# Cross-attention of a two-layer decoder: score rounds of the filling in neighbouring pairs, and the last eleven shifted rounds in turn on two pairs of PSUM banks

## The reference

```
Q = (layernorm(x) @ Wq).heads   K = (ctx @ Wk).heads   V = (ctx @ Wv).heads
scores = einsum('bhqd,bhkd->bhqk', Q, K) * 0.25
attn = softmax(scores, axis=-1)
x = x + einsum('bhqk,bhkd->bqhd', attn, V).reshape(B, T, 256) @ Wo
```

## Time and profile before

| | |
|---|---|
| median of 3 runs | 1474.68 us (1469.47 to 1475.07) |
| profiled execution | span 1473.2 us from its first to its last instruction; a time of its own around the span is not given |
| cross-attention of layer 0 | 153.1 to 491.9 us |
| its first score round, first shifted round, last values | 163.5, 197.2, 479.4 us |
| cross-attention of layer 1 | from 942.0 us on |
| its first score round, first shifted round, last values | 952.2, 972.1, 1264.7 us |
| mean granted clock of PE | 0.911 |

### The profile page before, as it was taken

How to read it: one execution, slowest core, us unless ns; L and a number is a source line. 1 busy time by engine, 2 the same in 40 slices (tenths; PEclk the granted TensorE clock), 3 DMA queues, 4 the chain that set the end, 5 groups by cost and what they waited for, 6 DMA issues and landing times. The chain is left out here.

```text
span 1473.2 us, 34595 instructions
## 1 busy us (share of the span) xinstructions
PE 1305.0 (89%) x13568; PEld 1036.2 (70%) x13568; DVE 701.9 (48%) x1744; ACT 558.2 (38%) x1246; POOL 444.8 (30%) x654
## 2 busy tenths in 40 slices
PE   5998899999998389999994999799999998559996
PEld 2665457777776279999993777557777776459996
DVE  4885345555552612222222999545565552323322
ACT  2776035555554012222221555135555553112221
POOL 5994300000000155556552221200000000135662
PEclk8999579999998589999997999799999997569999
DMA  7000111111110369999984000011111110279994
GB/s 241 2 2 2 23 26 36 36 36 37 36 36 17 128 225 340 346 347 337 329 320 107 1 1 1 15 29 42 44 44 43 42 43 25 80 192 347 356 368 147
DMA packets 61355, 177.89 MB, mean 121 GB/s; under 512 B 20608, under 2 KB 41953, under 8 KB 46756
## 3 DMA queue, kind: packets, MB, share of 16 engines
q0 software_dynamic: 22176, 141.55, 27.0%
q1 hardware_dynamic: 39044, 34.46, 9.2%
HBM read 147.62 MB, written 12.85 MB: 109 GB/s over the span
## 5 line engine op out<-in xcount | busy, mean ns | idle before, releaser
L975 DVE TENSOR_REDUCE xa_mx<-xa_ps_s 112x2 f32<-112x750 f32 x246 | 231.5, 941 | 219.4 <-PE xa_ps_s L704 215.9
L892 ACT ACTIVATE xa_p<-xa_ps_p 125x672 f32<-125x672 f32 x256 | 187.2, 731 | 236.2 <-PE xa_ps_p L710 236.2
L710 PEld LDWEIGHTS xa_ps_p<-xa_qT,xa_kT 32*125 32x125 f32 x3072 | 199.4, 191 | 95.3 <-ACT xa_p L892 66.8
L710 PE MATMUL xa_ps_p<-xa_qT,xa_kT 32*125 32x112 f32 x3072 | 243.4, 291 | 24.4 <-DVE xa_mx L975 10.4
L704 PE MATMUL xa_ps_s<-xa_kT,xa_qT 32*112 32x375 f32 x984 | 224.8, 534 | 1.0 <-DMA xa_qT<-xa_qU 1.0
L1803 PEld LDWEIGHTS ex_ps_h<-ex_xT,ew_w 128*128 128x128 f32 x1792 | 213.7, 196 | 4.8 <-issue 2.0
L1803 PE MATMUL ex_ps_h<-ex_xT,ew_w 128*128 128x128 f32 x1792 | 214.3, 279 | 1.3 <-ACT ex_xT L1833 1.3
L1814 PE MATMUL ex_ps_y<-ew_w,ex_hT 128*128 128x256 f32 x896 | 202.7, 379 | 0.0
L1814 PEld LDWEIGHTS ex_ps_y<-ew_w,ex_hT 128*128 128x128 f32 x896 | 165.9, 190 | 20.2
L1837 ACT ACTIVATE ex_hT<-ex_ps_h,ew_w 128x128 f32<-128x128 f32 x224 | 70.1, 364 | 282.5 <-PE ex_ps_h L1803 282.5
L1849 DVE TENSOR_SCALAR ex_hT<-ex_ps_h,ew_w 128x128 f32<-128x128 f32 x224 | 68.2, 346 | 163.7 <-PE ex_ps_h L1803 163.7
(11 more groups left out here) (304 smaller groups left out, 2000.0 us busy)
## 6 DMA issues: line engine op xcount, KB each, us to landing
xa_kT<-xa_kU SPq DMA_DIRECT2D x128, 93.8 KB, 2.2
xa_qT<-xa_qU SPq DMA_DIRECT2D x64, 56.0 KB
xn<-xa_x SPq DMA_DIRECT2D x32, 112.0 KB, 2.2
lin_yg<-ys SPq DMA_DIRECT2D x16, 224.0 KB, 5.2
cT<-in_ctxT SPq DMA_DIRECT2D x4, 750.0 KB, 8.3
xa_qT<-xa_nmT SPq DMA_DIRECT2D x128, 1.8 KB
x<-in_x SPq DMA_DIRECT2D x4, 448.0 KB, 6.2
xn<-x SPq DMA_DIRECT2D x16, 112.0 KB, 2.1
```

Of the source, the lines that this page charges most:

```text
L710: return pe.matmul(bp[0:CT, i, c * S:(c + 1) * S], kT[r:r + 32, b % RB, n, c * CT:(c + 1) * CT], qT[r:r + 32, b % RB, n, :], start=True, s ...
L892: act.activation(p[slot % 4][:, :, :], bp[0:CT, :, 0:NC3 * S], ACT.Exp).then_inc(exped, 1)
L975: dve.tensor_reduce(mx[:, b % 2, j:j + 2, n], score_banks(b, pair)[0:S, :, 0:CL], AX, ALU.max).then_inc(maxed, 1)
```

## The change

Three edits and what they need:

1. **Filling.** `round_of` loses its branch without shifted rounds. The loop over t starts at 0, and the filling is written out ahead of it: `fill_round` in pairs 0 and 1, 2 and 3, and so on, with the other products between the pairs, and no identity product behind a round. `keys(0, 1)` stands ahead of the first round and of the five or nine identity products, which stay. On DVE `normed_row(1)` comes before the first maximum and `q_copy(1)` before the maximum of pair 4.
2. **Drain.** From round DRAIN = 117 on, the shifted rounds take `bsc` and `bp` in turn (`shifted_banks`) and wait for the exponential of two rounds before. Round 117 also waits for all 128 maxima.
3. **Zeros.** `spread_q` waits for `q_copied` behind its DMA of zeros instead of ahead of it.

```diff
+    DRAIN = PAIRS * NB - FILL
...
+    def shifted_banks(t, slot):
+
+        r = PAIRS * t + slot
+        return bsc if r >= DRAIN and (r - DRAIN) % 2 == 0 else bp
...
             def spread_q(b):
-                sp.wait_ge(q_copied, b + 1)
                 reused(sp, shifted, PAIRS * (b - RB + 1))
...
                 sp.dma_start(qT[1:P:32, b % RB, :, :], zeros[:, :, :]).then_inc(q_spread[b % RB], 16)
+                sp.wait_ge(q_copied, b + 1)
...
             def round_of(t, slot):
...
-                    reused(pe, exped, PAIRS * t + slot)
+                    r = PAIRS * t + slot
+                    if r == DRAIN:
+                        pe.wait_ge(maxed, PAIRS * NB)
+                    reused(pe, exped, r - 1 if r >= DRAIN else r)
...
-                elif on(sb):
-                    if sb == 0 and sp == 0:
-                        pe.wait_ge(br_set, 1)
-                    idle_products(bm[:, 0:P], 1)
+
+            def fill_round(b, pair):
+                if pair == 0:
+                    pe.wait_ge(q_spread[b % RB], 16 * Q_DMAS)
+                if pair % 4 == 0:
+                    pe.wait_ge(k_spread[RB * (pair // 4) + b % RB], 16 * K_DMAS)
+                reused(pe, maxed, PAIRS * b + pair - 1)
+                score(b, pair, 0)
+                score(b, pair, 1).then_inc(scored, 1)
...
             keys(0, 0)
-            for t in range(-3, NB + 2):
+            x_turn(0)
+            queries(0)
+            keys(0, 1)
+            bias_rows()
+            idle_products(bp[:, 0, 0:P], 5 + 4 * layer)
+            fill_round(0, 0)
+            fill_round(0, 1)
+            x_turn(1)
+            keys(1, 0)
+            fill_round(0, 2)
+            fill_round(0, 3)
+            queries(1)
+            fill_round(0, 4)
+            fill_round(0, 5)
+            context_values(0, 0)
+            context_values(0, 1)
+            fill_round(0, 6)
+            fill_round(0, 7)
+            context_values(0, 2)
+            keys(1, 1)
+            shift_turn(0)
+            for pair in range(FILL - PAIRS):
+                fill_round(1, pair)
+            x_turn(2)
+            for t in range(NB + 2):
...
-                act.activation(p[slot % 4][:, :, :], bp[0:CT, :, 0:NC3 * S], ACT.Exp).then_inc(exped, 1)
+                act.activation(p[slot % 4][:, :, :], shifted_banks(t, slot)[0:CT, :, 0:NC3 * S], ACT.Exp).then_inc(exped, 1)
...
+                    if t == -2 and slot == 4:
+                        normed_row(1)
+                    if t == -1 and slot == 1:
+                        q_copy(1)
...
-                    if slot == 1 and on(t + 2):
+                    if slot == 1 and on(t + 2) and t != -1:
...
-                    if slot == 6 and on(t + 3):
+                    if slot == 6 and on(t + 3) and t != -2:
```

More of the change, by code:

```diff
@@ L709, in shifted_score @@
                 r = 32 * j
-                return pe.matmul(bp[0:CT, i, c * S:(c + 1) * S], kT[r:r + 32, b % RB, n, c * CT:(c + 1) * CT],
+                return pe.matmul(shifted_banks(b, pair)[0:CT, i, c * S:(c + 1) * S], kT[r:r + 32, b % RB, n, c * CT:(c + 1) * CT],
                                  qT[r:r + 32, b % RB, n, :], start=True, stop=True)
@@ L844, in _ @@
                     values(t - 1, 3)
-                if on(t + 2) and t > -2:
+                if on(t + 2):
                     keys(t + 2, 0)
@@ L849, in _ @@
                     queries(t + 2)
-                    if t == -2:
-                        bias_rows()
-                        idle_products(bp[:, 0, 0:P], 5 + 4 * layer)
                 round_of(t, 2)
```

## The result

The changed kernel takes 1426.47 us (median of 4 runs, 1424.82 to 1427.28), the kernel before in the runs beside it 1472.08 us (4 runs); ratio 0.9699, 95% interval 0.966 to 0.9738. The profiled execution took 1427.28 us, its span is 1425.5 us: 47.7 us less than before.

The account below looks back on a forecast made before the run. PE was taken to bound layer 0's filling, at half clock. Gains of 16.3 + 5.7 + 5 + 10 = 37.0 us off a 1473.2 us span, plus 1.5 us to the median, gave 1437.7 us, range 1427 to 1454.

Parts of the forecast that it names:

- The filling of layer 0: Layer 0 up to the first shifted round: clock rises, DVE then bounds; 17.2 us gained, 16.3 after one slow round.
- The filling of layer 1: Layer 1 up to the first shifted round: 966.3 against 972.06, a gain of 5.7 us.
- the start at 951.9: Layer 1's first score round: zeros issued sooner remove its 0.98 us wait for query DMAs, so it starts at 951.9.
- The drains: Last shifted rounds of both layers: waits of 0.83 us go and the clock holds longer; 5 us and 10 us gained.
- If the clock falls at the same 469.4 us: Drain of layer 0: case where the clock still drops at that time; last values start at 474.3, gaining 5.1 us.
- Up to round 120: Drain of layer 0: round 120 waits for its shift DMAs, so only 0.5 us is won up to there.
- all at 2.4 GHz is 12.4 us of work: Drain of layer 0 behind round 120: with the clock held, last values start at 472.1 instead of 479.4, gaining 7.3 us.
- The chain behind the drains: Copy, turn, normalise, project, second norm and logits behind the last values: only start sooner, no further gain counted.
- The zero for the steady stretch: Steady rounds: query DMAs land long before their round, so zero gain; one slow round, 0.9 us, taken off in layer 0.
- The rivals at 1.2 GHz (fillings or drains): Fillings stay at 1.2 GHz: 1446.2 us, chance 0.15; or drains give only their waits: 1449.6 us, chance 0.18.
- the one without overlap: Fillings: neighbouring rounds follow one another and layer 0 stays at 1.2 GHz; 1448.5 us, chance 0.04.
- the slower one: Rounds behind the fillings stay at 1.2 GHz after a longer shift-DMA wait; gain gone after 41 rounds; chance 0.07.

Follow-up runs that it names:

- hold_no_lead: Changed kernel with identity products in PE's waits at the filling's end, without the five or nine ahead of the first pair: 1418.73 us, ratio 0.9699.
- zeros_back: Changed kernel with the wait for the query copy again ahead of the DMA of zeros: 1428.08 us, ratio 0.9762 to the kernel before.
- drain_only: Kernel before with the drain's edit alone, its fillings unchanged: 1439.58 us, ratio 0.9837.
- fill_only: Changed kernel with its drain undone, the last eleven shifted rounds on one pair of banks: 1452.78 us, ratio 0.9917 to the kernel before.
- hold: Changed kernel with identity products in PE's waits at the filling's end and between the first two shifted rounds: 1424.92 us, ratio 0.9753 to the kernel before.
- after_again: Changed kernel run again unaltered, in another group: 1428.77 us, ratio 0.9744 to the kernel before.

## Why the prediction was right, and where it was not

**The filling of layer 0** was forecast at 17.2 us and gave 19.3. The path was the one named: the clock rises, then DVE bounds it (8.4 us from the first maximum to the shift row, 8.5 counted), then 5.4 us to the first shifted round (5.0 counted). Mis-sized was its start: the second keys, counted as 1.4 us of delay, were offset by identity products and a bias row at 2.4 GHz, since the clock rose ahead of the first pair and not behind it. The first score round began 10.05 us behind the first keys, 10.40 in the kernel before; and the first maximum followed after 0.93 us, not 1.64. The reason that I gave, five identity products *and* products side by side, was more than is needed: in hold_no_lead the clock rose behind the first pair with no identity products ahead of it.

**The filling of layer 1** was forecast at 5.7 us and gave 4.4. The failed step is the start at 951.9: I let the wait for the query DMAs go, but put nothing there for the moved keys, and the first score round came 10.81 us behind the first keys where it had come 10.19. zeros_back shows that the zeros had nothing to give. The sum of the steps behind it was 0.5 us short (14.9 us measured, 14.4 counted).

**What I did not see** is that the kernel before has two outcomes. I read the one trace as if layer 0 were slow and layer 1 fast by nature, and as if nine identity products had lifted the clock in layer 1; drain_only has it the other way round with the same filling, at 0.50 behind those nine. That the two terms come so near is in part luck: one slow filling in two is what the two traces of this code (before, drain_only) happen to show, and the terms rest on which execution was profiled.

**The drains** were forecast at 5 and 10 us and gave 7.6 and 15.7. The mechanism stood (no wait of 0.83 us is left, and without them the clock holds 1.00), the size did not: "If the clock falls at the same 469.4 us" was the case I leaned on in layer 0, and in 15 of 16 new drains it did not fall before the last values. Up to round 120 0.5 us was won, as counted. The step that all at 2.4 GHz is 12.4 us of work held (12.15 us from round 120 to the last values), by two errors that cancel: neighbouring rounds run side by side, which I had counted in series, and the value products then wait 0.51 us, which I had not.

**The chain behind the drains** was counted as starting sooner and no more; it gave 3.7 and 3.4 us on top, for 2.4 us of each because its products too ran at the higher level for a part (0.79 up to the logits, against 0.50 in fill_only, where the last logits start 11.95 us behind the last values instead of 9.52). The other 1.3 and 1.0 us lie in stages behind the logits whose code is the same, and stay open.

**The zero for the steady stretch** was wrong in layer 0, which lost 6.8 us where 0.9 was taken off. The first two shifted rounds take 7.04 us, 2.2 more than before, and 4.82 in hold, where the waits ahead of them are filled. Most of the rest, 4.4 us, lies between rounds 112 and 117 (14.75 us against 10.38): the late key DMA and the 6.8 us at 0.50 that follow. after_again, where PE waits 0.51 us there and the clock stays, loses 3.5 us. Other traces of old and new fillings have the wait too, so it is no part of the change. My trace of before just lacked it.

The DMA is not issued late; it lands late. Each half of a batch's keys goes in two DMAs:

```profile
q8 instruction: 1, 0.02, 1.6%
xa_kT<-xa_kU SPq DMA_DIRECT2D x2, 93.8 KB, 3.2
```

These are lines of the DMA view of the changed kernel in 425 to 432 us: one packet on the queue for instructions, and the median of the two DMAs from issue to landing, 3.2 us where it is 2.2 over the whole trace of before. The second of them was issued by 427.02 us and landed 3.73 us later, and a packet of 16384 bytes for instructions was under way from 427.75 to 429.53 us. Of the 1374 key DMAs whose landing the fourteen traces have, 46 landed more than 2.5 us behind the end of their issue (median 1.6 us), and all 46 had such a packet under way in their first 1.6 us, as had 280 of the other 1328. So the loading of code goes with the delay, and whether a round is hit depends on where the two fall. By what path one delays the other no run shows.

By terms: +2.1 and -1.3 us in the fillings, +2.6 and +5.7 in the drains, +7.1 behind them, -5.5 in the steady stretches: 10.7 us, from 37.0 to the 47.7 measured on the spans. The rivals at 1.2 GHz (fillings or drains) and the one without overlap fell with the granted clocks above; the slower one had its mechanism, slow rounds behind the filling, for two rounds per layer and not for 41, and behind a wait for the shift DMAs that was shorter than the old one of layer 1 (0.91 us against 1.68).

The Trainium skill (TensorE: Matmul & The Clock Gate, section A second HAM failure mode: psum-queue depth-cycling) tells of a kernel that goes round its banks with small idle times of PE and swings between the levels. The filling of layer 0 goes round its banks too, with 2.73 of 14.77 us idle, and holds 1.00; the trace does not agree with the page there. At the filling's end, and in the old drains, the clock falls behind waits of 0.3 to 1.0 us, and as far as the fall goes the traces agree. The same page (section The mechanism) says that products on different row groups overlap; the first pair agrees: two rounds in 0.83 us.

## What to carry to other kernels

Where PE stands between two clock levels, take more than one trace of a stretch before pricing it: the same instructions took 19.9 or 33.8 us here. Where PE waits just under a microsecond several times in a stretch with little other work, the waits are the smaller part of the price: filling them with products that nobody reads gave about 6.7 us per drain on average, taking them away 3.4 us more. Overlapped products can save nothing, as in these drains, if what follows waits for another engine anyway.

## What the runs showed of the hardware

- PE's busy time does not decide its clock: 33.72 busy of 33.75 us at 0.50, 12.04 of 14.77 us at 1.00, with the same score products in both, 32 rows deep. In drain_only the same filling stood at 1.00 in one layer and at 0.50 in the other.
- In fillings that began at 0.50, rounds in neighbouring pairs had the clock up within 6.3 us (eight of eight); rounds one behind the other did not within 24.6 us (three of three).
- The clock can fall behind waits of at most 1.03 us. Eight products of 128 x 128 in those three waits, and five behind the first shifted round, kept it at 1.00 from 162.2 to 462.5 us (hold, layer 0), in layer 1 from 923.3 to 1189.6 us.
- All 46 key DMAs that landed over 2.5 us behind their issue had a 16384-byte packet for instructions under way.
- The kernel before varied over 33.6 us between 17 runs, the changed one over 10.0 us between 6 beside it. Two outcomes of a filling (13.9 us apart) and old drains of 24.8 to 33.4 us fit that spread; no trace of one of the longest runs shows it.
